# Four products for the second band too, with row sums and half of the pooling moved to accumulating transfers issued by GpSimd

## What is computed

```python
def _predictor_mask(x):
    pooled = x.reshape(B, C, H // 8, 8, W // 8, 8).mean(axis=(3, 5))
    m = pooled >= 0.05
    return repeat(m, 8 in both directions)
mask = _predictor_mask(x)
x_high = where(mask, x, 1e-5)
x_low = where(mask, 1e-5, x)
y_high = conv(quant_act_uint(x_high, act_scale_high, 8), quant_weight_per_oc(w_high, 8))
y_low = conv(quant_act_uint(x_low, act_scale_low, 4), quant_weight_per_oc(w_low, 4))
return y_high + y_low
```

## Time and profile before

| | |
|---|---|
| median of 3 runs | 652.44 us (650.45 to 653.19) |
| the profiled execution | 653.09 us, of which the span of the trace is 651.3 us |
| TensorE busy | 626.5 us, 96% of the span |
| VectorE busy | 593.7 us, 91% |
| ScalarE busy | 483.9 us, 74% |
| GpSimd busy | 9.7 us, 1% |
| transfers | 104.07 MB, 41.9% of the 16 DMA engines' span |

### The profile page before, as it was taken

The page is one execution under the profiler, slowest core; times in us unless marked ns, Lnnn a source line. Parts: engine busy times, 40 slices in busy tenths (PEclk is TensorE's granted clock), DMA queues, the critical chain, the costliest instruction groups (busy, mean ns, idle before and its releaser), DMA issues.

```text
span 651.3 us, 10766 instructions
## 1 busy us (share of the span) xinstructions
PE 626.5 (96%) x3714; PEld 360.8 (55%) x3714; DVE 593.7 (91%) x805; ACT 483.9 (74%) x491; POOL 9.7 (1%) x30
## 2 busy tenths in 40 slices
PE   3779999999999999999999999999999999999996
PEld 1345555555555555555555555555555555555554
DVE  7889999999999999999999999999999999999933
ACT  6669877787787787787778778777778877877542
POOL 3200000000000000000000000000000000000000
PEclk9889999999999999999999999999999999999999
DMA  6244555334355433445543434553343554331122
GB/s 270 99 156 142 199 199 197 150 123 177 141 197 197 184 126 142 182 155 197 197 154 125 172 148 190 197 194 129 139 179 148 197 197 160 129 162 63 78 99 100
DMA packets 14409, 104.07 MB, mean 160 GB/s; under 512 B 1728, under 2 KB 1728, under 8 KB 10432
## 3 DMA queue, kind: packets, MB, share of 16 engines
q1 hardware_dynamic: 14400, 103.95, 41.9%
HBM read 52.56 MB, written 51.38 MB: 160 GB/s over the span
## 4 chain that ended last, share of the span: by engine, by line
PE 95%; ACT 2%; DVE 1%; DMA 1%; issue 0%; DVEq 0%; SPq 0%
PE psum L335 95%; DMA wraw_l<-w_low 1%; ACT rounded_h L449 0%; ACT psum L484 0%; ACT wT_l L466 0%; DVE pooled L618 0%; PE psum L321 0%; DVE w_max_l L577 0%; ACT wT_h L466 0%; DVE ybuf L712 0%; DVEq L63 0%; DVE wq_l L600 0%; DVE wint_l L584 0%; DVE upper L696 0%; DVE wq_l L589 0%
## 5 line engine op out<-in xcount | busy, mean ns | idle before, releaser
L484 ACT ACTIVATE psum<-psum,ratio 128x1344 f32<-128x1344 f32 (+2 forms) x159 | 174.4, 1097 | 123.7 <-PE psum L335 122.7
L335 PE MATMUL psum<-plane_l,wT_l 128*128 128x448 f16 (+1 forms) x1164 | 207.8, 328 | 0.0
L335 PE MATMUL psum<-plane_h,wT_h 128*128 128x448 f16 (+1 forms) x1164 | 205.5, 326 | 0.0
L335 PEld LDWEIGHTS psum<-plane_l,wT_l 128*128 128x128 f16 x1164 | 114.3, 98 | 77.8 <-issue 3.0
L335 PEld LDWEIGHTS psum<-plane_h,wT_h 128*128 128x128 f16 x1164 | 113.4, 98 | 76.6 <-issue 1.7
L712 DVE SCALAR_TENSOR_TENSOR ybuf<-psum,out_scale_h,shared 128x448 f32<-128x448 f32 (+1 forms) x194 | 111.2, 601 | 20.0 <-PE psum L335 9.7
L618 DVE TENSOR_REDUCE pooled<-xbuf 128x49 f32<-128x3136 f32 (+2 forms) x33 | 109.3, 3313 | 0.0
L449 ACT ACTIVATE rounded_l<-xbuf,inv_act_l 128x1568 int16<-128x1568 f32 (+1 forms) x64 | 101.7, 1592 | 4.5 <-DMA xbuf<-x 4.5
L505 ACT ACTIVATE shared<-psum,bias,out_scale_h 128x448 f32<-128x448 f32 (+1 forms) x128 | 86.3, 674 | 23.2 <-PE psum L335 22.6
L449 ACT ACTIVATE rounded_h<-xbuf,inv_act_h 128x1568 int16<-128x1568 f32 (+1 forms) x64 | 101.9, 1594 | 0.0
L335 PE MATMUL psum<-rowsum_l,wT_l 128*128 128x448 f16 (+1 forms) x384 | 87.2, 336 | 2.3 <-ACT wT_l L466 2.3
(11 more groups left out here) (76 smaller groups left out, 340.6 us busy)
## 6 DMA issues: line engine op xcount, KB each, us to landing
xbuf<-x SPq DMA_DIRECT2D x31, 1568.0 KB, 6.6
y<-ybuf SPq DMA_DIRECT2D x32, 896.0 KB, 3.6
y<-ybuf SPq DMA_DIRECT2D x32, 672.0 KB, 4.0
xbuf<-x SPq DMA_DIRECT2D x1, 896.0 KB, 7.6
xbuf<-x SPq DMA_DIRECT2D x1, 672.0 KB, 5.0
wraw_l<-w_low SPq DMA_DIRECT2D x1, 576.0 KB, 3.8
wraw_h<-w_high SPq DMA_DIRECT2D x1, 576.0 KB, 5.9
act_scales<-scales SPq DMA_DIRECT2D x1, 1.0 KB, 1.8
```

The lines of the kernel that those rows point to most:

```text
L335: last = nc.tensor.matmul(out, wT[k][:, mat, :], moving(k, p, band, row, dx), start=(k == "l" and j == 0), stop=(j == len(parts) - 1), ski ...
L484: return nc.scalar.activation(banks, banks, ACT.Identity, scale=ratio[:, 0:1])
```

## The change

Band 1 joins `FAST`, so it takes four products like band 3. That adds its differences and its four-instruction drain on VectorE, its scaling in two pieces on ScalarE, and on TensorE a wait before M2 of the low branch for the `lower` tile of the fast band before it, which read the same bank.

The row sums leave VectorE from image 1 on. GpSimd issues two transfers for each branch: one copies the odd rows of the plane (d1) to `rowsum`, and one adds the rows d2 to it (`accum_op=ALU.add`). The second waits until the first has landed.

The pooling from image 2 on reads a new buffer `halves` of half the size. Two more transfers of GpSimd fill it from x in HBM: one copies rows 0 to 3 of every block of 8 rows, one adds rows 4 to 7. VectorE then reduces 1568 elements a partition, not 3136. `xbuf` is still loaded for the rounding.

On ScalarE `shared` of band 0 moves ahead of the scaling of band 1, and the two pieces of the high rounding stand together behind `shared` of band 1. On VectorE the two output rows of band 1 are no longer split around the differences. `wint` is now one tensor for both branches.

```diff
-    FAST = (3,)
+    FAST = (1, 3)
...
+            def begin_halves(m, p):
+
+                pool.wait_ge(s_pooled, prepared(m - 2))
+                nc.gpsimd.dma_start(halves[:, bass.ds(p, 1), :, :], image_halves(m)[:, :, 0, :]).then_inc(s_half, 16)
+
+            def add_halves(m, p):
+                pool.wait_ge(s_half, 16 * (m - 1))
+                nc.gpsimd.dma_start(halves[:, bass.ds(p, 1), :, :], image_halves(m)[:, :, 1, :], accum_op=ALU.add
+                                    ).then_inc(s_halves, 16)
+
+            def begin_row_sums(k, m, p):
+                pool.wait_ge(s_plane[k], 2 * prepared(m))
+                nc.gpsimd.dma_start(rowsums[k][:, bass.ds(p, 1), :], planes[k][:, bass.ds(p, 1), ODD:ODD + SUMS]
+                                    ).then_inc(s_rows_copied[k], 16)
+
+            def add_row_sums(k, m, p):
+                pool.wait_ge(s_rows_copied[k], 16 * m)
+                nc.gpsimd.dma_start(rowsums[k][:, bass.ds(p, 1), :], planes[k][:, bass.ds(p, 1), PITCH:PITCH + SUMS],
+                                    accum_op=ALU.add).then_inc(s_rows_summed[k], 16)
...
+            begin_halves(2, 0)
+            add_halves(2, 0)
+            with pool.Fori(1, B - 2) as m:
+                p = m % 2
+                begin_row_sums("l", m, p)
+                begin_halves(m + 2, p)
+                begin_row_sums("h", m, p)
+                add_row_sums("l", m, p)
+                add_row_sums("h", m, p)
+                add_halves(m + 2, p)
...
                 elif band == 0:
-                    pe.wait_ge(signal, prepared(n))
+                    pe.wait_ge(s_rows_summed[k], 16 * n)
...
                     products("l", p, band, "M1")
+                    if not (early(n) and band == FAST[0]):
+
+                        pe.wait_ge(s_lower, fast_index(n, band))
                     products("l", p, band, "M2").then_inc(s_low_inner, 1)
...
+                shared_tile(n, 0)
                 low_scaled(n, 1)
-                shared_tile(n, 0)
+                shared_tile(n, 1)
                 if ahead > 1:
                     quantise("h", i + 1, p, 0)
-                shared_tile(n, 1)
-                if ahead > 1:
                     quantise("h", i + 1, p, 1)
...
+                    dve.wait_ge(s_halves, 16 * (n - 1))
+                    blocks = halves[:, p, :, :].rearrange("p a (y b x) -> p a b y x", b=BX, x=POOL)
...
                     apply_mask("l", m, mp)
                     apply_mask("h", m, mp)
-                    row_sums("l", m, mp)
...
                 out_rows(n, p, 0)
                 if ahead > 0:
-                    row_sums("h", m, mp)
-                out_row(n, p, 1, 0)
+                    differences("l", m, mp, 1)
+                out_rows(n, p, 1)
                 if ahead > 0:
                     differences("l", m, mp, 3)
-                out_row(n, p, 1, 1)
-                if ahead > 0:
+                    differences("h", m, mp, 1)
                     differences("h", m, mp, 3)
```

More of the change, by code:

```diff
@@ L78, in conv_program @@
         clipped = {k: sb(f"clipped_{k}", [P, HW], F16) for k in "hl"}
-        plane = {k: [sb(f"plane_{k}{p}", [P, PLANE], F16) for p in range(2)] for k in "hl"}
-        rowsum = {k: [sb(f"rowsum_{k}{p}", [P, SUMS], F16) for p in range(2)] for k in "hl"}
+        planes = {k: sb(f"plane_{k}", [P, 2, PLANE], F16) for k in "hl"}
+        plane = {k: [planes[k][:, p, :] for p in range(2)] for k in "hl"}
+        rowsums = {k: sb(f"rowsum_{k}", [P, 2, SUMS], F16) for k in "hl"}
+        rowsum = {k: [rowsums[k][:, p, :] for p in range(2)] for k in "hl"}
         outer = {k: {b: [sb(f"outer_{k}{b}{p}", [P, 2, BAND[b][1] * PITCH + 2], F16) for p in range(2)] for b in FAST} for k in "hl"}
@@ L83, in conv_program @@
                  for k in "hl"}
+        halves = sb("halves", [P, 2, BY, POOL // 2 * W], F32)
         pooled = sb("pooled", [P, BY * BX], F32)
@@ L94, in conv_program @@
         wraw = {k: sb(f"wraw_{k}", [P, TAPS, C], F32) for k in "hl"}
-        wint = {k: sb(f"wint_{k}", [P, TAPS, C], I16) for k in "hl"}
+        wint = sb("wint", [P, TAPS, C], I16)
         wq = {k: sb(f"wq_{k}", [P, MATS, C], F16) for k in "hl"}
@@ L148, in conv_program @@
         s_rowsum = {k: sem(f"rowsum_ready_{k}") for k in "hl"}
+        s_rows_copied = {k: sem(f"row_sums_begun_{k}") for k in "hl"}
+        s_rows_summed = {k: sem(f"row_sums_landed_{k}") for k in "hl"}
+        s_half = sem("upper_halves_landed")
+        s_halves = sem("halves_landed")
         s_low = sem("low_product")
@@ L348, in low @@
                 new = not (first_image(n) and band < 2)
-                wait_prepared(s_rowsum["l"], n, band)
+                wait_prepared("l", n, band)
                 if new:
@@ L373, in high @@
                 g = BANDS * n + band
-                wait_prepared(s_rowsum["h"], n, band)
+                wait_prepared("h", n, band)
                 if fast(n, band):
@@ L613, in pool_blocks @@
                 a0, a1 = (0, BY) if q is None else PART[q]
-                if first_image(n) and q == 0:
-                    dve.wait_ge(s_x_start, 16)
-                else:
-                    dve.wait_ge(s_x[p], 16 * i + 16)
-                nc.vector.tensor_reduce(
-                    pooled[:, a0 * BX:a1 * BX].rearrange("p (a b) -> p a b", b=BX),
-                    xbuf[p][:, elements(q)].rearrange("p (a y b x) -> p a b y x", y=POOL, b=BX, x=POOL),
-                    AX.XY, ALU.add).then_inc(s_pooled, 1)
+                if early(n):
+                    if first_image(n) and q == 0:
+                        dve.wait_ge(s_x_start, 16)
+                    else:
+                        dve.wait_ge(s_x[p], 16 * i + 16)
+                    blocks = xbuf[p][:, elements(q)].rearrange("p (a y b x) -> p a b y x", y=POOL, b=BX, x=POOL)
+                else:
+                    dve.wait_ge(s_halves, 16 * (n - 1))
+                    blocks = halves[:, p, :, :].rearrange("p a (y b x) -> p a b y x", b=BX, x=POOL)
+                nc.vector.tensor_reduce(pooled[:, a0 * BX:a1 * BX].rearrange("p (a b) -> p a b", b=BX), blocks,
+                                        AX.XY, ALU.add).then_inc(s_pooled, 1)
             def choose(n, q=None):
@@ L757, in body @@
                     apply_mask("l", m, mp)
-                    row_sums("l", m, mp)
                     out_rows(n, p, 2)
                     apply_mask("h", m, mp)
-                    row_sums("h", m, mp)
                     out_rows(n, p, 3)
                     for k in "lh":
-                        differences(k, m, mp, 3)
+                        for band in FAST:
+                            differences(k, m, mp, band)
                     return
```

36 lines of the change are left out of this document (22 added, 14 removed).

## The result

The changed kernel takes 719.38 us (median of 4 runs, 718.39 to 722.47), the kernel before 652.66 on the same chip (4 runs, 650.45 to 653.19). The ratio is 1.104, with a 95% interval of 1.101 to 1.106: 10.4% slower. The forecast was 621 with a range of 614 to 680: the direction was wrong, and the time lies outside the range. The profiled execution took 718.39 us, its span is 716.7.

What follows compares the result with a forecast made beforehand. The prediction took TensorE to bound the kernel, an image falling from 19.20 to 18.04 us. Its sum was 653.1 - 36.0 + 4.2 (start) = 621.3, given as 621 us, range 614 to 680.

Steps and rivals of the forecast that it cites:

- the transfers' amount: DMA engines, per image: 6.5 MB with adds counted once take 15.3 to 16.7 us, 85% to 93% of 18.04.
- T = 20.9: Upper end, in us an image, of the DMA engines' need if adds count twice (19.2 to 20.9).
- its own formula: Total time if the DMA engines need T us an image: 621 + 31 x (T - 18.04).
- Rival B: Adds count twice, so TensorE waits for row sums at every low 0: 657 to 710 us; chance 0.22.
- B's point of decision: DMA time an image from which the kernel is slower: 19.05 us, a rate under 427 GB/s for 8.1 MB.
- The transfers' latency: Row sums by copy, then add: 2.8 to 3.8 us each to land, no cost in the loop.
- The start: Image 1's low row sum, its add behind the high copy, comes 3.2 to 6.3 us late; 4.2 taken.
- The price of an issue: GpSimd issuing a pooling half of 896 pieces: 2.5 to 5.0 us; queue occupied 6.4 to 12.8 us an image.
- The wait for `lower`: TensorE before M2 of the low branch: 1.3 us in hand, so it costs nothing.
- Rival C: Issues of 896 pieces over 8 us make GpSimd's queue set the pace: 745 us at 10 us; chance 0.13.
- Rival A's tax on VectorE: VectorE 5% slower beside GpSimd, 16 us in all; its rival, 630 to 649 us, has chance 0.20.

Runs made afterwards that it cites:

- the best kernel: Changed kernel with row sums added by GpSimd's own instruction, placed behind VectorE's differences, pooling moved up, image 1's row sums on VectorE: 619.11 us, ratio 0.951.

## Why the prediction was wrong

**The step that failed: the transfers' amount.** It counted 6.5 MB an image at the rate at which bytes land, 15.3 to 16.7 us, and took "once" for the adds, "since a row of the trace only prices bytes that land". That is no reason: a price per landed byte from copies holds for copies. The measured price of an add is 2.08 copies over both kinds (estimated 1.8 in long packets, 2.5 in pieces of 896 bytes), and the amount 22.8 us of share time an image, which at the share of 1.07 takes 21.3. The Trainium skill ("Collectives: The Full Stack", section "The bandwidth ceiling") has an add at half the rate of a copy; the runs agree, at 1/2.08. The prediction quoted the rule and left the sum as it was. The whole result hung on this choice, since with T = 20.9 its own formula gave 710.

**Rival B was what happened.** Its upper end was T = 20.9 and 710 us; T measured 20.95, with which its formula gives 711. The loop has 30 periods and not 31, which takes 2.9 off, and the start adds 10.0 more than forecast: 718. That T came so near is luck in part. B put 8.1 MB at a rate read at a share of 0.43; the engines' time was 22.8 us, more than that, and they passed it at a share of 1.07, which brought it down again. B's point of decision, 19.05, is not contradicted: with 19.37 the kernel without additions was 1.0% slower than before, though more of that came from its start (56.94 against 50.13) than from its periods (30 x 0.16 = 4.8 us).

**The transfers' latency was mis-sized as well.** Per transfer 2.8 to 3.8 us were estimated from transfers in a loop at a share of 0.43. The medians measured are 4.0 and 5.5 (low and high) without the halves, 5.3 and 7.7 without additions, 6.6 and 10.1 in the changed kernel. Copy and add of the high branch had 15.8 us and can take 17.4 even as two copies. So with "once" the loop would have come to 19.37 us an image and the time to some 655 to 663, not 621. Of the 2.91 us an image by which the forecast missed (20.95 - 18.04), 1.33 stand in the kernel without additions and 1.58 come from the second read. The split goes by one profiled execution each, and that without additions was among the longer ones of its kernel. The first part is put down to landing time rather than amount, since the engines were at 0.90 to 0.96 there; that is argued, not tested. How much of it would be left if the halves were issued at another time was not tried.

**The start** was 14.2, not 4.2 us. The first add after the pipeline's start meets load, store and the pooling's halves. VectorE had waited too, and TensorE starts slowly:

```profile
45.22 1.79 DVE L674 TENSOR_REDUCE pooled<-halves 128x49 f32<-128x1568 f32 x1 [6.97 <-DMA halves<-x]
...
64.37 1.28 PE L384 MATMUL psum<-rowsum_l,wT_l 128*128 128x448 f16 x3 [16.11 <-issue]
...
69.22 0.74 PE L384 MATMUL psum<-rowsum_l,wT_l 128*128 128x448 f16 x3
```

The reduction waits 6.97 us for its first halves. TensorE stands for 16.11 us, and then three matmuls take 1.28 us where they take 0.74 otherwise, at the lower of the clock's two levels, 1.2 GHz; the granted clock is 0.57 from 50 to 60 us, in which TensorE did nothing, 0.50 from 64.3 to 66, and 0.79 from 60 to 80. The pair with and without image 1's row sums on VectorE shows 11.5 us of such a start, but without the halves; in the changed kernel itself the start was not taken apart.

**The price of an issue** was put too high: 2.5 to 5.0 us for 896 pieces, measured 0.96 for the copy and 1.68 for the add, 0.57 and 0.88 for 128 pieces. GpSimd's queue is occupied for 5.6 us an image and not 6.4 to 12.8. Rival C is out.

**What was right.** TensorE 18.04 us an image (18.06 wherever the transfers are in time), VectorE 17.67 (17.70), ScalarE 15.5 (15.35), the reduction 1.78 (1.781 by shape). The wait for `lower` cost nothing. Rival A's tax on VectorE by GpSimd's issues was not seen as such: in the kernel without pooling transfers VectorE took what was summed. And 621 us less its 4.2 for the start, 617, is near what the four products give once the row sums have another place: the best kernel here that computes everything takes 619.1.

## What to carry to other kernels

Before work moves from an engine to the DMA engines, sum their share time an image with an accumulating transfer at two copies (more if its pieces are short), and compare it with the new, shorter period, not the old one. Then price the chain: behind the pooling's half and another chain of copy and add the median of one of these transfers was 10.1 us, where a quiet trace had suggested 2.8 to 3.8, and with fewer transfers beside it 4.0 to 5.5. If an idle engine can do the work itself, put its instruction where the neighbour reads PSUM or a single SBUF tensor: the same add gave 744 us in one place and 619 in another.

## What the runs showed of the hardware

- An accumulating transfer takes 2.08 times the DMA engines' time of a copy (an estimated 1.8 in long packets, 2.5 in pieces of 896 bytes), and the profile counts its landed bytes once: 302 to 309 GB/s at a share of 1.06 to 1.08, against 449 for loads.
- Pieces of 896 bytes in place of 6272 cost 9% of the queue's time (425.7 against 387 us). Plain copies of the same pieces leave few packets under 2 KB (5632 against 32032).
- Two chains of copy and add at a DMA share of 1.07 land in 6.6 and 10.1 us a transfer, a single one at the same share in 5.4.
- GpSimd's add of 1626 elements takes 2.89 us beside VectorE's drains and 4.35 when it starts just behind a masking with two SBUF inputs. Differences that start during the add take 2.15 and 3.09 where they take 0.63 and 0.39. The masking, which had started first, kept its 1.86.
- Issues by GpSimd and some of VectorE's instructions hold each other up, by a few tenths. In the changed kernel one threshold took 0.56 beside the issue of an add, another 0.19:

```profile
314.43 1.69 POOL L330 DMA_DIRECT2D halves<-x  x1
314.85 0.56 DVE L683 TENSOR_SCALAR chosen<-pooled 128x49 f16<-128x49 f32 x1
...
335.65 0.19 DVE L683 TENSOR_SCALAR chosen<-pooled 128x49 f16<-128x49 f32 x1
```

  In the best kernel the second clip beside an issue took 1.35 in place of 1.03, and the issue 1.59 in place of 0.96. By the Trainium skill ("SBUF — State Buffer", section "SBUF: two separate sides") GpSimd cannot write its descriptors while VectorE holds the port that they share; the trace agrees for the clip, and shows the reverse too: VectorE's instruction gets longer as well.
